# Four-layer kernel on one core: expert transfers issued by three engines, and 32-column tiles in the second layer of the pairwise network

## The reference

```python
# mixture of experts: 64 experts, 4 of them per row, FE = 64
_, topk_idx = top_k(flat @ router_w + router_bias, 4)
g = silu(einsum('nd,edf->nef', flat, wg)); u = einsum('nd,edf->nef', flat, wu)
routed = einsum('ne,nef,efd->nd', comb, g * u, wd)
# sparse attention: a network on all pairs of rows chooses 51 keys for each
h = einsum('bsd,fd->bsf', xn, W1)                                  # f = 128
pair = relu(h[:, :, None, :] - h[:, None, :, :] + b1)
pair = relu(einsum('bijf,gf->bijg', pair, W2) + b2)                # layer two, g = 64
sim = einsum('bijg,og->bijo', pair, W3)[..., 0] + b3[0]            # layer three
```

## Time and profile before

| | us |
|---|---|
| median of 3 runs | 2911.58 |
| lowest, highest run | 2882.16, 2920.47 |
| the profiled execution | 2894.68 |
| its span | 2892.9 |
| PE busy in it | 2511.6 (87%) |
| DVE, ACT, POOL busy | 1764.9, 1092.9, 461.1 |
| mean granted clock of PE | 0.873 |

### The profile page before, as it was taken

The page is one execution under the profiler, slowest core; times in us unless marked ns, Lnnn a source line. Parts: engine busy times, 40 slices in busy tenths (PEclk is TensorE's granted clock), DMA queues, the critical chain, the costliest instruction groups (busy, mean ns, idle before and its releaser), DMA issues. The chain is left out here.

```text
span 2892.9 us, 41665 instructions
## 1 busy us (share of the span) xinstructions
PE 2511.6 (87%) x11963; PEld 856.4 (30%) x11963; DVE 1764.9 (61%) x4678; ACT 1092.9 (38%) x1303; POOL 461.1 (16%) x778
## 2 busy tenths in 40 slices
PE   7996856555207999999999999999989999999996
PEld 3445544434103222222222222222212222222224
DVE  4555311111256888888888888888756554556655
ACT  4551011111004554454454445544524333344442
POOL 0001701111442122222222222222100000000001
PEclk9996966767658999999999999999959866789998
DMA  7001244445325000000000000000000000000000
GB/s 291 3 1 47 102 148 148 146 147 154 118 65 159 0 0 0 0 0 0 0 0 0 0 0 0 0 0 0 0 19 16 12 12 9 14 11 15 12 4 29
DMA packets 116945, 121.58 MB, mean 42 GB/s; under 512 B 15088, under 2 KB 100080, under 8 KB 116848
## 3 DMA queue, kind: packets, MB, share of 16 engines
q1 hardware_dynamic: 105584, 86.85, 10.0%
q0 software_dynamic: 11264, 33.57, 3.3%
HBM read 64.79 MB, written 55.57 MB: 42 GB/s over the span
## 5 line engine op out<-in xcount | busy, mean ns | idle before, releaser
L1369 PE MATMUL spre<-sunit,w2t 128*64 128x512 f32 x4096 | 937.8, 600 | 10.4 <-DVE sunit L1263 10.4
L1263 DVE TENSOR_SCALAR sunit<-hneg,sshift 128x512 f32 x2048 | 843.6, 482 | 27.1 <-POOL sshift L1249 24.8
L1335 ACT ACTIVATE sunit<-spre,b 128x1024 f32<-128x1024 f32 x512 | 570.5, 1114 | 595.4 <-PE spre L1369 595.4
L1667 DVE CUSTOM_DVE_ANT_0 bjunk<-bs,bmask_s 128x512 bf16<-128x512 f32 x512 | 347.0, 691 | 246.8 <-PE bs L1505 226.1
L1369 PEld LDWEIGHTS spre<-sunit,w2t 128*64 128x64 f32 x4096 | 272.1, 137 | 664.4 <-issue 638.8
L1617 ACT ACTIVATE bpt<-bs 128x1024 f32<-128x1024 f32 x256 | 262.0, 1023 | 435.9 <-PE bs L1525 435.9
L1254 POOL COPY swindow<-bands 128x32 f32 x256 | 184.9, 722 | 888.5 <-PE ssims L1379 888.4
L1379 PE MATMUL ssims<-sunit,swindow 128*32 128x512 f32 x2048 | 272.8, 605 | 0.0
L1505 PE MATMUL bs<-bks,bqs 32*128 32x512 bf16 x512 | 226.0, 445 | 15.3 <-DVE bpeaks L1667 9.3
L1525 PE MATMUL bs<-mask_t,identb 128*128 128x512 bf16 (+1 forms) x512 | 222.5, 435 | 0.0
L1523 PE MATMUL bs<-bqm,bks 32*128 32x512 bf16 x512 | 219.5, 429 | 0.5 <-DVE bqm L1690 0.5
(11 more groups left out here) (281 smaller groups left out, 2224.9 us busy)
## 6 DMA issues: line engine op xcount, KB each, us to landing
slot_rows<-blank SPq DMA_DIRECT2D x4, 4096.0 KB, 26.0
exin<-slot_rows SPq DMA_DIRECT2D x64, 256.0 KB, 3.0
slot_out<-eyout POOLq DMA_DIRECT2D x64, 256.0 KB, 2.9
ewg<-L_ffn_wg SPq DMA_DIRECT2D x128, 64.0 KB, 1.9
ewu<-L_ffn_wu SPq DMA_DIRECT2D x128, 64.0 KB, 1.9
ewd<-L_ffn_wd SPq DMA_DIRECT2D x128, 64.0 KB, 2.2
q_parts<-pfill SPq DMA_DIRECT2D x4, 1024.0 KB, 8.6
k_parts<-pfill SPq DMA_DIRECT2D x4, 1024.0 KB, 11.3
```

Source lines behind the costliest of these rows:

```text
L1263: ve.tensor_scalar(unit1[:, u, j, :], k.hneg[:, bass.ds(b * S, S)], shift[:, u, j // 2, j % 2:j % 2 + 1], 0.0, ALU.add, ALU.max).then_inc( ...
L1335: act.activation(unit2[:, v, 2 * h:2 * h + 2, :], pre[:, h, :, :], ACT.Relu, bias=b2[:, 0:1]).then_inc(hidden, 1)
L1369: mm = pe.matmul(pre[s * KW:(s + 1) * KW, h, c % 2, :], k.w2t[:, :], unit1[:, u, 2 * c + s, :], start=True, stop=True)
L1667: ve.tensor_tensor_reduce(junk[:, n % 2, :], s1[:, n % 2, :], mask_s[:, q, :], 1.0, GONE, ALU.add, ALU.max, peaks[:, q, c:c + 1]).then_inc ...
```

## The change

Transfers of the pairs. The gate and up weights of an expert lie in one array `gate_up` in HBM (64 x 128 x 256), and SP issues one transfer for both. SP waits for the gate product of pair m-4 (`p_up`) instead of the down product, and issues nothing else. POOL issues the down weights of both experts as one indirect DMA (128 rows of 256 f32, by row numbers `down_rows` that DVE computes from the owners), after waiting for the down product of pair m-4, and then the rows of the pair. ACT issues the store of pair m-2 after its two activations. The owner product has 128 columns instead of 32.

Layer two of the pairwise network. Each matmul with 64 columns becomes two with 32 columns, at column positions 0, 32, 64 and 96.

```diff
@@ block.sync of experts
-            sp.wait_ge(owners_kept, 1)
+            gur = i["gate_up"].rearrange("e p n -> p e n")
+            sp.wait_ge(owners_kept, 3)
             for m in range(PAIRS):
                 r = m % RING
                 if m >= RING:
-                    sp.wait_ge(p_down, m - RING + 1)
+                    sp.wait_ge(p_up, m - RING + 1)
                 for e in range(2):
                     one = bass.ds(sp.value_load(owner[0:1, 2 * m + e:2 * m + e + 1], min_val=0, max_val=EXPERTS - 1), 1)
-                    sp.dma_start(wg[:, r, e, :, :].rearrange("p c f -> p (c f)"), wgr[:, one, :].rearrange("p e n -> p (e n)")).then_inc(gate_up_in[r], 16)
-                    sp.dma_start(wu[:, r, e, :, :].rearrange("p c f -> p (c f)"), wur[:, one, :].rearrange("p e n -> p (e n)")).then_inc(gate_up_in[r], 16)
-                    sp.dma_start(wd[e * FE:(e + 1) * FE, r, :], wdr[:, one, :].rearrange("f e d -> f (e d)")).then_inc(down_in[r], 16)
-                if m == 0:
-                    sp.wait_ge(scattered, 16 * TILES * TOPK)
-                sp.dma_start(xin[:, r, :, :],
-                             xs[2 * m * P:(2 * m + 2) * P, :].rearrange("(e p) d -> p e d", p=P)).then_inc(rows_in[r], 16)
+                    sp.dma_start(wgu[:, r, e, :, :, :].rearrange("p w c f -> p (w c f)"),
+                                 gur[:, one, :].rearrange("p e n -> p (e n)")).then_inc(gate_up_in[r], 16)
@@ block.gpsimd of experts
+            down_table = i["L0_ffn_wd"].rearrange("e f d -> (e f) d")
+            pool.wait_ge(owners_kept, 3)
             for m in range(PAIRS):
-                pool.wait_ge(p_out, m + 1)
-                pool.dma_start(ys[2 * m * P:(2 * m + 2) * P, :].rearrange("(e p) d -> p e d", p=P),
-                               yout[:, m % RING, :, :]).then_inc(stored[m % RING], 16)
+                r = m % RING
+                if m >= RING:
+                    pool.wait_ge(p_down, m - RING + 1)
+                pool.indirect_dma_start(
+                    out=wd[:, r, :], out_offset=None, in_=down_table,
+                    in_offset=bass.IndirectOffsetOnAxis(ap=down_rows[:, m:m + 1], axis=0)).then_inc(down_in[r], 16)
+                if m == 0:
+                    pool.wait_ge(scattered, 16 * TILES * TOPK)
+                pool.dma_start(xin[:, r, :, :],
+                               xs[2 * m * P:(2 * m + 2) * P, :].rearrange("(e p) d -> p e d", p=P)).then_inc(rows_in[r], 16)
@@ route, on DVE
-            ve.tensor_scalar(owner[:, :], owner_at, -1.0, None, ALU.add).then_inc(owners_kept, 1)
+            ve.tensor_scalar(owner[:, :], owner_at[0:1, :], -1.0, None, ALU.add).then_inc(owners_kept, 1)
+            for z in range(2):
+                half = slice(z * FE, (z + 1) * FE)
+                ve.tensor_scalar(down_rows[half, :], owner_at.rearrange("p (m e) -> p m e", e=2)[half, :, z], float(FE),
+                                 lane[half, :], ALU.mult, ALU.add).then_inc(owners_kept, 1)
@@ block.scalar of experts
-            for m in range(PAIRS + 1):
+            for m in range(PAIRS + 2):
...
-                if m:
+                if 0 < m <= PAIRS:
...
+                if m >= 2:
+                    a = m - 2
+                    act.wait_ge(p_out, a + 1)
+                    act.dma_start(ys[2 * a * P:(2 * a + 2) * P, :].rearrange("(e p) d -> p e d", p=P),
+                                  yout[:, a % RING, :, :]).then_inc(stored[a % RING], 16)
@@ second_layer of pairwise
                 for c in range(2 * h, 2 * h + 2):
-                    for s in range(2):
-                        mm = pe.matmul(pre[s * KW:(s + 1) * KW, h, c % 2, :], k.w2t[:, :], unit1[:, u, 2 * c + s, :],
-                                       start=True, stop=True)
+                    for g in range(4):
+                        mm = pe.matmul(pre[32 * g:32 * g + 32, h, c % 2, :], k.w2t[:, 32 * (g % 2):32 * (g % 2) + 32],
+                                       unit1[:, u, 2 * c + g // 2, :], start=True, stop=True)
```

More of the change, by code:

```diff
@@ L535, in experts @@
         ones = sb("ones", [P, TILES])
-        ones_row = sb("ones_row", [EXPERTS, 32])
+        ones_row = sb("ones_row", [EXPERTS, P])
         logit = sb("logit", [P, TILES, EXPERTS])
@@ L545, in experts @@
         tiles_wide, begun = sb("tiles_wide", [EXPERTS, P]), sb("begun", [EXPERTS, P])
-        owner = sb("owner", [32, P], I32)
+        owner, lane, down_rows = sb("owner", [1, P], I32), sb("lane", [P, 1]), sb("down_rows", [P, PAIRS], I32)
         base = sb("base", [P, EXPERTS])
@@ L554, in experts @@
         xin = sb("xin", [P, RING, 2, D])
-        wg, wu = sb("wg", [P, RING, 2, C, FE]), sb("wu", [P, RING, 2, C, FE])
+        wgu = sb("wgu", [P, RING, 2, 2, C, FE])
         wd = sb("wd", [P, RING, D])
@@ L572, in experts @@
         begun_at = bank[0:EXPERTS, ROUTE, 192:192 + P]
-        owner_at = bank[0:32, OWNER, 0:P]
+        owner_at = bank[:, OWNER, 0:P]
         @block.sync
@@ L617, in _ @@
                       allow_small_or_imprecise_dtypes=True).then_inc(made, 1)
-            pool.wait_ge(made, 8)
+            pool.iota(lane[:, :], [[1, 1]], base=-FE, channel_multiplier=1,
+                      allow_small_or_imprecise_dtypes=True).then_inc(made, 1)
+            pool.wait_ge(made, 9)
+            pool.iota(lane[FE:P, :], [[1, 1]], base=-FE, channel_multiplier=1,
+                      allow_small_or_imprecise_dtypes=True).then_inc(made, 1)
+            pool.wait_ge(made, 10)
             pool.affine_select(out=before[:, :], in_=before[:, :], compare_op=ALU.is_ge, fill=0.0, base=-1,
@@ L661, in route @@
                 ve.max(best[:, t, :], ranked[:, t, :]).then_inc(step, n.up())
-            ve.wait_ge(made, 9)
+            ve.wait_ge(made, 11)
             ve.wait_ge(step, n.now())
@@ L845, in gate_pair @@
             r = m % RING
-            pe.wait_ge(gate_up_in[r], 64 * (m // RING + 1))
+            pe.wait_ge(gate_up_in[r], 32 * (m // RING + 1))
             pe.wait_ge(p_kept, m + 1)
@@ L849, in gate_pair @@
                 pe.wait_ge(p_hidden, m - 1)
-            for w, z in ((wg, 0), (wu, 1)):
+            for z in range(2):
                 for c in range(C):
@@ L853, in gate_pair @@
                         mm = pe.matmul(bank[e * FE:(e + 1) * FE, GATE_BANKS[m % 2], z * P:(z + 1) * P],
-                                       w[:, r, e, c, :], pxt[:, m % 2, e, c, :], start=c == 0, stop=c == C - 1)
+                                       wgu[:, r, e, z, c, :], pxt[:, m % 2, e, c, :], start=c == 0, stop=c == C - 1)
             mm.then_inc(p_up, 1)
@@ L859, in down_pair @@
             r = m % RING
-            pe.wait_ge(down_in[r], 32 * (m // RING + 1))
+            pe.wait_ge(down_in[r], 16 * (m // RING + 1))
             pe.wait_ge(p_hidden, m + 1)
@@ L908, in _ @@
             pe.wait_ge(added, 2 * B)
-            pe.wait_ge(owners_kept, 1)
+            pe.wait_ge(owners_kept, 3)
             turn_pair(pe, 0)
@@ L1943 @@
 INPUTS = ["L0_attn_x", "L0_attn_Wq", "L0_attn_bq", "L0_attn_Wk", "L0_attn_bk", "L0_attn_Wv", "L0_attn_bv",
[L1944 removed]
+          "L0_attn_Wo", "L0_attn_bo", "L0_ffn_router_w", "L0_ffn_router_bias",
           "L0_ffn_wd", "L0_ffn_swg", "L0_ffn_swu", "L0_ffn_swd", "L1_attn_gamma", "L1_attn_beta", "L1_attn_W1",
@@ L1956 @@
     arrays, aps = {}, {}
-    for name in INPUTS:
-        a = np.ascontiguousarray(inputs[name])
+    laid_out = {name: inputs[name] for name in INPUTS}
+    laid_out["gate_up"] = np.concatenate([np.reshape(inputs["L0_ffn_" + w], (EXPERTS, P, C * FE)) for w in ("wg", "wu")], axis=2)
+    for name in laid_out:
+        a = np.ascontiguousarray(laid_out[name])
         arrays[name] = a
```

3 lines of the change are left out of this document (removed).

## The result

| | before | after |
|---|---|---|
| median of the runs, same chip (us) | 2896.87 (4 runs, the three shown above and one more; 2856.9 to 2920.47) | 2720.38 (4 runs, 2715.38 to 2725.43) |
| profiled execution / its span (us) | 2894.68 / 2892.9 | 2718.49 / 2716.7 |
| mean granted clock | 0.873 | 0.894 |

The changed kernel takes 0.948 of the time before (95% interval 0.940 to 0.956). Some runs of a kernel come out longer at a lower granted clock; the medians here count them, the ratios leave them out. The profiled executions are 176.2 us apart; the prediction had 212.

What follows compares the result with a forecast made beforehand. PE was taken to bound the pairwise stage, and issue, landing and PE in series the expert pairs. From 2894.7 us, less 72, 138 and 2, came 2683, put at 2695 for a median; range 2645 to 2795.

Steps and rivals of the forecast that it cites:

- layer two: Pairwise stage: 32-column tiles remove the width changes, 0.29 us of each 4.58 us step; 72 us saved, bounds 0 to 80.
- pairs' pace x 63: Expert pairs: 3.9 us a pair instead of 6.09, saving 138 us, with ends of 157 and 100.
- start and small edits: Before the pairs: second row transfer earlier, 2 us saved; owner product and index rows cost nothing, under 1 us if uncovered.
- rival A: Layer two: width change isn't what costs 0.29 us, or doubled instructions eat the gain; only pairs gain, 2755 us; 10%.
- D: Pairwise stage: PE's issue of 80 instructions a step becomes the bound, up to 3535 us; 4%.
- DVE's wait: Pairwise stage: wait ahead of L1290 for the tile before falls from 10.7 to about 6 us a tile.
- The order of the ring: Expert pairs: rows issued 1.55 us after the down product, 3.2 to land, then PE's burst of 4.2 or 2.4 us.
- the landing: Expert pairs: from POOL's issue of the rows to PE's start, 3.2 us, up to 4.2 for the range.
- one of the signs named for a wrong prediction: PE issue gaps in layer two, ACT's store ahead of turned rows over 3.6 us, or rows landing after over 4.2 us.
- Rival B: Expert pairs: rows land only behind the gather in POOL's queue, 5.5 us after issue; 5.6 us a pair, 2793 us; 12%.
- Rival C: Expert pairs: no gain, since the DMA engines are shared and transfers bind the ring; 2823 us; 4%.
- ScalarE's store: Expert pairs: store's issue on ACT 0.58 us; ACT's round 2.9 us, at worst 3.9, hides under 3.9 a pair.

Runs made afterwards that it cites:

- the experiment with two widths: Changed kernel with the first half of each step's layer two in 64-column tiles, the second in 32: steps of 4.59 us, 2865.73 us in one run.
- the best version: Changed kernel with POOL issuing the rows after the gate product of pair m-4, before its wait for the down product and the gather: 2631.89 us, ratio 0.915.
- rows ahead of the gather: Changed kernel with POOL issuing a pair's rows before the gather of its down weights, under the old wait: 2725.18 us, ratio 0.934.
- rows on SP: Changed kernel with SP issuing the rows after its wait for the gate product, ahead of its weights; POOL has the gather alone: 2714.39 us, ratio 0.922.
- gate and up once: Changed kernel with gate and up weights loaded for the first four pairs only: 2756.43 us, ratio 0.940.
- its near twin: Changed kernel with SP issuing the rows once pair m-4 is turned, only the weights waiting for the gate product: 2654.36 us, ratio 0.918.

## Why the prediction was right, point by point

The forecast was 2695 us in 2645 to 2795, and the median is 2720. Against the profiled execution 212 us were forecast and 176 came; the terms:

| term, us saved | forecast | measured |
|---|---|---|
| layer two | 72 | 69.6 |
| pairs' pace x 63 | 138 (100 to 157) | 97.5 |
| start and small edits | 2 | 3.6 (4.3 sooner, 0.7 later) |
| after the pairwise stage | 0 | 5.6 |

**Layer two** was right in mechanism, price and neighbour. The nearest row gave the 0.43 us for each group of four; the experiment with two widths refutes the first half of rival A, and 80 instructions in 4.29 us, 54 ns each, refute D: the weight loads come on the array's beat. DVE's wait was to be about 6 us a tile and is 7.5: it is shorter by 3.2 us for 4.6 us less of PE. Another 0.9 us a tile went from DVE's idle time ahead of layer one, which fell from 27.1 to 13.0 us in all (part 5 of the two pages), most of it a wait for POOL's shift columns; the prediction had put the whole 4.6 to the one wait.

**The order of the ring** was right: a down product, a gather's issue, rows, landing, burst. In the kernel before, SP itself was nearly full besides: between 400 and 740 us it waited for a down product 28 times, 47.6 us in all, 0.8 us a pair, so shorter landings alone could have given little more than that. The time from the down product to the rows was 1.22 us, less than the 1.55 forecast, since no pause of 0.30 follows the gather; a clock above 0.69 came too (0.85). **The mis-sized term is the landing.** The prediction took 3.2 us from the timeline of a kernel with a DMA share of 0.49, and gave 4.2 as its end; rows to PE was 4.80, and the landing itself 4.6, so one of the signs named for a wrong prediction did appear. The means over pairs 4 to 63 give the account of two pairs: 1.24 to the rows' issue (1.55 forecast), 4.91 from there to PE (3.2), 3.09 of burst (about 3.0, which the forecast of 3.9 a pair implies). Of the 1.7 us in the middle 1.3 is the landing (4.53 in the mean) and 0.4 a term that the prediction didn't have: PE still busy with the other pair's burst when the rows are there. Together two pairs cost 1.4 us more than forecast, 0.7 each, over 40 us in 63. So the saving of the pairs (97.5) missed even its cold end (100). That the total stayed in the range is in part luck of its width: the range was drawn to take in A and B, and landings only up to 4.2 us.

What the runs put in its place is two causes, each of which the prediction had in a rival and priced wrong. Rival B had the rows landing behind the gather at 5.5 us, 2.3 above the forecast: swapping the two takes 0.6 us off rows to PE and 0.4 off the landing, with the share going the other way, so this part is some 0.4 us or more, and not 2.3. Rival C had the DMA engines shared, which the prediction itself costed as "every us costs 0.5 us a pair, 32 in all": taking 256 KB out takes 0.8 us off rows to PE, 0.7 where PE waited. How the rise from 3.03 splits isn't settled further, since the queue's order and the share can't be changed one at a time in a running ring.

**Issue from several engines.** The page "DMA: Bandwidth & Descriptors" of the Trainium skill, section "Issuing engines are not separate DMA queues", says that several issuing engines save only issue time. Here the edits of the transfers (three issuers, four transfers for seven, an earlier wait on SP) took the issue ahead of the rows from 4.5 to 1.2 us and the pair from 5.98 to 4.52 us, since issue stood in the chain, so its "usually small" doesn't hold for this ring. How much of that the sharing alone gives wasn't run. Its first part, that all share the same 16 engines, fits the best version: 0.93 share and 3.04 us a pair, the same as with the rows issued by SP.

**ScalarE's store** was costed at 0.58 us of issue, and takes 0.37. It did stand ahead of the turned rows at times, but PE's gate product, which reads them, has 0.0 us of idle time ahead of it in the page (L869): it never bound. POOL has 0.98 + 0.77 = 1.75 us a pair, below 2.3. The owner product and the two index rows cost nothing that can be seen: the first row transfer came 4.3 us sooner, not later.

## What to carry to other kernels

When several engines wait on one resource, follow the ring from release to release and write each issue, landing and burst beside it: only what stands in it counts, and the transfer that closes it goes first in its queue, released by the earliest reader that frees its buffer and not by the last. A landing read at a low DMA share (3.0 us at 0.49) is too short a price once the change raises that share (4.6 at 0.65, behind a gather): reprice it with the bytes a pair over the new pace. Where tiles of a TensorE stage alternate in width, count the changes (0.29 us for two here) before the instructions, since doubling the instructions cost nothing here.

## What the runs showed that was not expected

**The same kernel differs by 80 us between chips.** The changed kernel took 2720 us on one chip and 2800 on another (2897 and 2943 before). Its pace in the pairs and its pairwise steps are the same. The stretch 290 to 330 us, where PE is at the shared experts beside POOL's scatters, is not the same; first the chip of the result, then the other:

```profile
290.00:310.00 20.00, 19.45 (x59) 10.83 (x58) 9.63 (x11) 2.39 (x4) 15.71 (x15) 1.00 0.24 98
310.00:330.00 20.00, 20.00 (x64) 11.81 (x63) 11.20 (x12) 2.39 (x4) 15.14 (x16) 1.00 0.24 98
```

```profile
290.00:310.00 20.00, 3.41 (x8) 1.15 (x7) 4.27 (x4) 0.60 (x1) 15.12 (x17) 0.70 0.24 98
310.00:330.00 20.00, 1.32 (x3) 1.17 (x4) 1.29 (x2) 0.00 (x0) 15.13 (x17) 0.50 0.26 106
```

PE, DVE and ACT almost stand still while POOL issues at the same pace. The first copy of the pairs comes at 421.5 instead of 367.2 us, 54 of the 78 us between the spans, and the rest lies behind the pairwise stage (814.4 instead of 787.6 us). That last part goes with the granted clock, on every chip: in the profiled executions of all versions, whose program is the same there, it lasts from 764 us at 0.85 (rows ahead of the gather) over 788 at 0.81 (changed kernel) to 821 at 0.77 (rows on SP). What sets the clock there isn't shown, but the 57 us between the ends are more than half the saving of the pairs, and they are in every total. The versions with layer two or the transfers alone, rows ahead of the gather, gate and up once, rows on SP and the one of two widths, which ran on the same two chips, have late first copies too (404 to 425 us); the later ones, on two further chips, don't (366 to 373). The delay isn't the same for both kernels: layer two alone, with the old transfers, has 404 against 376 in the kernel before, and the transfers alone 419 against 367 in the changed one. Each of these is one profiled execution; if the others are like them, this takes 24 us from the gain of the transfers on that chip, most of what their total missed. A late supply of instructions would look like this; no run tests it, so the cause is open. These differences are why totals were compared by ratio and parts by their own pace: "rows on SP" is at 2714 us and its near twin at 2654, with ratios of 0.922 and 0.918.

**Issue prices.** A plain transfer of 256 KB costs the issuing queue 0.37 us on ACT, 0.58 on SP (0.45 where SP issues the rows ahead of its weights) and 0.77 on POOL; a gather of 128 rows costs POOL 0.98 us. A plain transfer behind the gather starts with no pause, a gather behind a plain transfer 0.30 us after it.
